# An attention kernel of two layers on one core: weights requested on another queue, fewer warm matmuls, new instruction orders

## The reference

```python
q = einsum('rc,bcn->brn', Wq, xf) + bq[None, :, None]     # 16 rows
k = einsum('rc,bcn->brn', Wk, xf) + bk[None, :, None]
v = einsum('oc,bcn->bon', Wv, xf) + bv[None, :, None]     # 128 rows
energy = einsum('bri,brj->bij', q, k)
attn = softmax(energy, axis=2)
out = einsum('bcj,bij->bci', v, attn)
x = gamma * out + x
```

## Time and profile before

| | |
|---|---|
| median of 3 runs | 193.89 us (193.38 to 194.21) |
| the profiled execution | 193.06 us |
| its span in the trace | 191.3 us |
| TensorE, ScalarE, GpSimd, VectorE busy | 94%, 81%, 82%, 76% of the span |
| DMA queue of SyncE | 9.31 MB, 16.7% of 16 engines' span |

### The profile page before, as it was taken

The page is one execution under the profiler, slowest core; times in us unless marked ns, Lnnn a source line. Parts: engine busy times, 40 slices in busy tenths (PEclk is TensorE's granted clock), DMA queues, the critical chain, the costliest instruction groups (busy, mean ns, idle before and its releaser), DMA issues.

```text
span 191.3 us, 3482 instructions
## 1 busy us (share of the span) xinstructions
PE 179.1 (94%) x1282; PEld 123.1 (64%) x1282; DVE 145.7 (76%) x137; ACT 155.5 (81%) x223; POOL 156.9 (82%) x120
## 2 busy tenths in 40 slices
PE   7889999799999989999998999999999999799993
PEld 2343445574798577877766786786668976565680
DVE  0258799868899898889878896798897867898241
ACT  2239969999999989999897998999998989348900
POOL 2267127989999999999999999999999976958760
PEclk9999999999999999999999999999999999999999
DMA  6920802200040040000400021003210101001111
GB/s 155 345 104 0 215 9 42 69 3 3 2 113 0 5 111 3 0 3 3 110 3 0 3 55 58 2 3 107 61 55 7 55 0 58 3 0 55 55 55 55
DMA packets 3890, 9.51 MB, mean 50 GB/s; under 512 B 548, under 2 KB 932, under 8 KB 3876
## 3 DMA queue, kind: packets, MB, share of 16 engines
q1 hardware_dynamic: 3876, 9.31, 16.7%
HBM read 2.89 MB, written 2.10 MB: 26 GB/s over the span
## 4 chain that ended last, share of the span: by engine, by line
PE 34%; POOL 31%; ACT 15%; issue 10%; DMA 4%; DVE 4%; SPq 1%; POOLq 0%; DVEq 0%; ACTq 0%
POOL attn_lo L364 14%; PE out_psum L720 10%; POOL attn_hi L359 9%; ACT ring L472 8%; PE out_psum L722 7%; ACT attn L484 4%; DMA qk_swapped<-qk 4%; PE ring L671 3%; PE ring L697 3%; PE out_psum L756 3%; PE ring L642 2%; DVE neg_max L563 2%; PE ring L624 2%; PE ring L657 2%; ACT attn_hi L490 2%
## 5 line engine op out<-in xcount | busy, mean ns | idle before, releaser
L364 POOL TENSOR_TENSOR attn_lo<-attn,attn_hi 128x1024 fp32r<-128x1024 f32 x37 | 90.4, 2455 | 1.8 <-ACT attn_hi L490 1.3
L563 DVE TENSOR_REDUCE neg_max<-ring 128x1 f32<-128x1024 f32 x64 | 75.6, 1219 | 15.7 <-PE ring L673 15.3
L472 ACT ACTIVATE ring<-ring,neg_max 128x1024 f32<-128x1024 f32 x64 | 69.6, 1087 | 9.9 <-DVE neg_max L563 9.3
L484 ACT ACTIVATE attn<-ring 128x1024 f32<-128x1024 f32 x64 | 63.3, 1024 | 9.8 <-DVE attn_lo L558 5.6
L359 POOL TENSOR_SCALAR attn_hi<-attn 128x1024 fp32r<-128x1024 f32 x35 | 39.2, 1134 | 5.5 <-ACT attn L484 5.4
L699 PE MATMUL ring<-qk_swapped,qk 64*128 64x512 f32 x64 | 29.0, 478 | 0.0
L697 PE MATMUL ring<-qk,qk_swapped 64*128 64x512 f32 x64 | 28.5, 468 | 0.3
L671 PE MATMUL ring<-qk_swapped,qk 64*128 64x512 f32 x56 | 25.1, 452 | 3.4 <-ACT attn L484 1.7
L673 PE MATMUL ring<-qk,qk_swapped 64*128 64x512 f32 x56 | 25.7, 461 | 0.0
L558 DVE TENSOR_TENSOR attn_lo<-attn,attn_hi 128x1024 fp32r<-128x1024 f32 x11 | 19.4, 1778 | 5.5 <-POOL attn_hi L359 4.7
L723 PE MATMUL out_psum<-attn_hi,v_hi 64*128 64x512 f32 x72 | 23.0, 399 | 0.0
(11 more groups left out here) (66 smaller groups left out, 358.1 us busy)
## 6 DMA issues: line engine op xcount, KB each, us to landing
qk_swapped<-qk SPq DMA_DIRECT2D x16, 256.0 KB, 3.7
out_dram<-x_all SPq DMA_DIRECT2D x8, 256.0 KB, 2.0
x_all<-x_in SPq DMA_DIRECT2D x3, 512.0 KB, 7.2
x_all<-x_in SPq DMA_DIRECT2D x2, 256.0 KB, 3.0
late<-late_in SPq DMA_DIRECT2D x1, 320.0 KB, 6.1
units<-units_in SPq DMA_DIRECT2D x1, 320.0 KB, 6.4
weights<-weights_in SPq DMA_DIRECT2D x1, 131.0 KB, 2.2
qk<-shift_rows SPq DMA_DIRECT2D x7, 8.0 KB
```

Of the source, the lines that this page charges most:

```text
L364: nc.gpsimd.tensor_tensor(attn_lo[:, k - 1], attn[:, k], attn_hi[:, k - 1].bitcast(fp32), ALU.subtract).then_inc(cut_made["lo", "gpsimd"], 1)
L472: nc.scalar.activation(e[:], e[:], ACT.Exp, bias=neg_max[s][:, i:i + 1], accum_out=row_sum[s][:, i:i + 1]).then_inc(sum_made, 1)
L484: nc.scalar.activation(attn[:, k], ring_tile("ET", s, k)[:].rearrange("p (a n) -> p a n", a=2), ACT.Exp).then_inc(attn_made, 1)
L563: nc.vector.tensor_reduce(neg_max[s][:, i:i + 1], ring_tile("E", s, i)[:], axis=AX.X, op=ALU.max, negate=True).then_inc(max_made, 1)
```

## The change

The request for the weights moves from SyncE's queue to ScalarE's, ahead of the loading of the activation table. `WARM_UP` goes from 10 to 5, and two of the eight `warm` words in the order have one pair in place of two. All five orders are new. The work is the same, but part of it changes engine:

| | GpSimd | ScalarE | VectorE |
|---|---|---|---|
| `hi` | 35 to 44 | 13 to 4 | |
| `lo` | 37 to 32 | | 11 to 16 |
| `v_hi` | 3 to 4 | 5 to 4 | |
| `v_lo` | 5 to 4 | | 3 to 4 |

In `POOL_ORDER`, the words from `parts.1.1` up to `parts.7.1` hold 28 `hi`, 29 `lo`, 3 `v_hi`, 4 `v_lo` before, and 33, 27, 2 and 3 after. In `DVE_ORDER`, those from `rows.1.1` to `rows.7.1` hold 5 `lo` and 2 `v_lo` before, 8 and 3 after. `PE_ORDER` has 7 E tiles between `shift.4.1` and `shift.5.1` before and 14 after, and behind `shift.7.1` 11 PH, 15 PV and 8 ET before, 9, 16 and 9 after.

```diff
-WARM_UP = 10
+WARM_UP = 5
...
 PE_ORDER = """
-raw.0.0.0 raw.0.1.1 E.0.6.2 QX.1.0.0 E.0.0.1 QK.1.0.0 E.0.7.2 warm.0.2 E.0.4.0 E.0.2.1 E.0.1.2 warm.0.2 E.0.3.0
-E.0.5.1 VX.0.0.2 warm.0.2 E.1.4.0 V.0.0.2 shift.0.0.1 warm.0.2 E.1.7.1 warm.0.2 QX.2.0.0 E.1.6.2 QK.2.0.0 warm.0.2
...
-shift.4.1.0 PH.3.3 E.5.2.0 PH.3.1 E.5.1.1 PV.3.3 PV.3.1 PV.3.2 QX.6.0.2 ET.4.3.0 QK.6.0.2 ET.4.2.1 PH.3.4 ET.3.7.0
-V.5.0.0 ET.4.0.1 PH.4.3 ET.4.6.2 PV.4.3 E.6.3.0 QX.7.0.1 shift.5.1.2 PV.4.0 ET.4.7.2 E.6.2.0 QK.7.0.1 PH.4.1 PH.4.2
...
-ET.6.7.1 ET.6.3.2 shift.7.1.0 PH.6.6 PH.6.4 PH.6.5 PH.6.3 PH.6.2 ET.7.3.0 ET.7.2.2 PV.6.2 PV.6.1 PV.6.3 PV.6.6
-PV.6.5 PV.6.4 ET.7.0.1 ET.7.1.0 ET.7.6.2 PV.6.7 PH.7.2 ET.7.5.1 ET.7.4.0 ET.7.7.2 PV.7.2 PH.7.3 PV.7.0 PH.7.1 PH.7.6
-PV.7.1 PV.7.3 PH.7.5 PH.7.4 PV.7.6 PV.7.5 PV.7.4 PV.7.7
+raw.0.0.0 raw.0.1.1 QX.1.0.2 E.0.2.0 QK.1.0.2 E.0.1.1 warm.0.2 E.0.6.2 E.0.7.0 E.0.0.1 warm.0.2 E.0.3.2 E.0.5.0
+E.0.4.1 warm.0.1 VX.0.0.2 E.1.4.0 V.0.0.2 shift.0.0.1 warm.0.2 E.1.5.1 warm.0.2 QX.2.0.0 E.1.0.2 QK.2.0.0 warm.0.1
...
+E.4.1.2 E.4.0.0 PV.2.5 PV.2.6 PV.2.4 PV.2.7 ET.3.0.1 ET.3.5.2 E.5.5.0 ET.3.4.1 PH.3.1 shift.4.1.2 PH.3.2 E.5.4.2
+ET.3.7.1 PV.3.2 PH.3.3 QX.6.0.0 E.5.6.1 ET.4.2.2 QK.6.0.0 PV.3.3 ET.4.1.2 PV.3.0 E.5.1.1 ET.4.3.2 PV.3.1 VX.4.0.0
+ET.4.0.2 V.4.0.0 ET.4.6.1 PH.3.6 E.5.2.2 PV.3.6 E.6.0.0 E.6.3.1 PV.3.7 E.6.1.2 PH.3.4 E.5.0.1 PH.3.5 E.5.7.0 PV.3.5
+PV.3.4 VX.5.0.2 ET.4.7.1 V.5.0.2 E.6.4.0 PH.4.3 E.5.3.1 PV.4.0 ET.4.5.2 E.6.7.0 PV.4.3 PH.4.1 E.6.2.2 PH.4.2 E.6.5.1
+PV.4.1 PV.4.2 QX.7.0.0 shift.5.1.2 QK.7.0.0 E.6.6.1 ET.4.4.2 PV.4.7 PH.4.6 ET.5.1.2 PV.4.6 ET.5.5.1 PH.4.4 ET.5.3.2
+ET.5.6.0 PH.4.5 ET.5.2.1 PV.4.4 shift.6.1.2 PV.4.5 ET.5.0.0 ET.5.4.2 ET.5.7.1 E.7.0.0 PV.5.0 ET.6.3.1 E.7.4.2 PH.5.1
...
+PV.5.4 E.7.2.0 E.7.1.1 PV.5.7 ET.6.6.2 PH.5.5 PV.5.6 PV.5.5 VX.7.0.0 ET.6.7.2 E.7.6.1 V.7.0.0 PH.6.6 PH.6.2 PH.6.4
+ET.6.5.2 shift.7.1.0 ET.6.1.1 PV.6.4 PV.6.7 PV.6.0 ET.7.5.0 ET.7.6.1 ET.7.4.2 PV.6.6 PH.6.5 PH.6.1 PV.6.5 ET.7.2.1
+ET.7.1.2 ET.7.7.0 PH.6.3 PV.6.1 PV.6.2 ET.7.0.2 ET.7.3.0 PV.6.3 PV.7.7 PH.7.6 PV.7.0 PH.7.3 PH.7.5 PH.7.4 PH.7.1
+PH.7.2 PV.7.1 PV.7.5 PV.7.3 PV.7.2 PV.7.4 PV.7.6
 """
 ACT_ORDER = """
-sum.0.6 evac.1.0 sum.0.0 sum.0.7 sum.0.4 sum.0.2 sum.0.1 sum.0.3 log.0.0 sum.0.5 sum.1.4 v_hi.0.0 log.0.1 sum.1.7
...
-sum.7.0 sum.7.4 sum.7.1 attn.5.4 sum.7.6 sum.7.3 attn.6.0 sum.7.2 attn.5.7 v_hi.6.0 attn.6.5 attn.6.2 sum.7.7
-attn.6.4 attn.6.1 attn.6.6 sum.7.5 log.7.1 hi.6.6 hi.6.4 attn.6.3 attn.6.7 attn.7.3 v_hi.7.0 attn.7.2 hi.7.2
-attn.7.0 attn.7.1 attn.7.6 attn.7.7 attn.7.5 attn.7.4 hi.7.5 hi.7.4
+evac.1.0 sum.0.2 sum.0.1 sum.0.6 sum.0.7 sum.0.0 sum.0.3 sum.0.5 log.0.0 sum.0.4 log.0.1 sum.1.4 sum.1.5 sum.1.0
+attn.0.1 attn.0.0 attn.0.3 attn.0.2 sum.1.3 attn.0.7 attn.0.4 sum.1.7 sum.1.1 sum.1.6 sum.1.2 sum.2.4 log.1.1
...
+v_hi.5.0 attn.4.4 sum.6.6 log.6.1 attn.5.1 attn.5.5 attn.5.3 attn.5.6 attn.5.2 attn.5.0 attn.5.7 attn.5.4 sum.7.0
+attn.6.3 sum.7.4 sum.7.5 sum.7.7 attn.6.2 sum.7.3 attn.6.0 v_hi.6.0 attn.6.4 sum.7.2 attn.6.6 sum.7.1 attn.6.7
+sum.7.6 log.7.1 attn.6.1 attn.6.5 attn.7.6 attn.7.4 attn.7.5 attn.7.1 attn.7.7 attn.7.0 attn.7.3 attn.7.2 hi.7.3
 DVE_ORDER = """
...
-max.6.6 finish.3.1 v32.5.0 max.6.3 rows.5.1 lo.4.2 max.6.2 mask.7.0 stack.7.0 finish.4.0 max.6.4 max.6.0 max.6.7
-max.6.5 max.6.1 finish.4.1 max.7.0 max.7.4 max.7.1 rows.6.1 max.7.6 max.7.3 finish.5.0 max.7.2 v32.6.0 lo.5.4
-max.7.7 v_lo.6.0 finish.5.1 max.7.5 v32.7.0 lo.6.5 rows.7.1 lo.6.6 lo.6.3 lo.6.4 finish.6.0 v_lo.7.0 lo.7.2
-finish.6.1 lo.7.6 lo.7.5 finish.7.0 finish.7.1
+max.0.2 max.0.1 max.0.6 max.0.7 max.0.0 max.0.3 max.0.5 max.0.4 max.1.4 rows.0.0 v32.0.0 max.1.5 max.1.0 mask.2.0
...
+v32.3.0 rows.3.1 max.4.5 max.4.6 max.4.2 lo.2.6 max.4.4 finish.2.0 mask.5.0 stack.5.0 max.4.7 max.4.1 max.4.0
+finish.2.1 max.5.5 rows.4.1 max.5.4 lo.3.6 max.5.6 mask.6.0 stack.6.0 max.5.1 finish.3.0 v32.4.0 max.5.2 max.6.3
+max.6.0 max.6.1 max.5.0 max.5.7 finish.3.1 max.6.4 v32.5.0 max.5.3 max.6.7 max.6.2 max.6.5 finish.4.0 rows.5.1
+max.6.6 mask.7.0 v_lo.5.0 stack.7.0 lo.4.4 lo.5.1 rows.6.1 finish.4.1 max.7.0 lo.5.3 max.7.4 max.7.5 max.7.7 lo.5.4
+finish.5.0 max.7.3 v32.6.0 max.7.2 max.7.1 v_lo.6.0 finish.5.1 max.7.6 v32.7.0 lo.6.6 rows.7.1 lo.6.2 lo.6.5
+v_lo.7.0 lo.6.1 finish.6.1 finish.6.0 lo.7.5 lo.7.1 lo.7.3 lo.7.4 finish.7.0 finish.7.1
 POOL_ORDER = """
-mask.1.0 stack.1.0 parts.0.0 parts.0.1 v_lo.0.0 hi.0.2 hi.0.3 hi.0.1 lo.0.2 lo.0.3 lo.0.1 parts.1.1 hi.0.6 lo.0.6
...
-hi.3.1 hi.3.2 lo.3.2 lo.3.3 parts.4.1 lo.3.1 hi.3.4 lo.3.4 lo.3.6 lo.3.5 hi.4.3 hi.4.2 v_lo.4.0 lo.4.3 hi.4.1
-parts.5.1 lo.4.1 v_hi.5.0 lo.4.6 lo.4.5 hi.5.1 hi.5.2 lo.4.4 hi.5.3 v_lo.5.0 lo.5.3 parts.6.1 lo.5.1 lo.5.2 hi.5.4
-hi.5.5 hi.5.6 lo.5.5 lo.5.6 hi.6.2 hi.6.1 hi.6.5 parts.7.1 lo.6.2 hi.6.3 lo.6.1 hi.7.3 lo.7.3 hi.7.1 lo.7.1 hi.7.6
-lo.7.4
+mask.1.0 stack.1.0 parts.0.0 parts.0.1 v_hi.0.0 v_lo.0.0 hi.0.1 hi.0.3 hi.0.2 lo.0.3 lo.0.2 hi.0.4 lo.0.4 parts.1.1
...
+hi.3.3 lo.3.2 hi.3.1 parts.4.1 hi.3.6 lo.3.3 lo.3.1 hi.3.5 hi.3.4 lo.3.4 hi.4.1 hi.4.2 lo.4.2 lo.3.5 v_lo.4.0 hi.4.6
+hi.4.3 lo.4.3 lo.4.1 lo.4.6 parts.5.1 hi.4.5 lo.4.5 hi.4.4 parts.6.1 hi.5.1 hi.5.3 hi.5.5 hi.5.2 hi.5.4 lo.5.2
+hi.5.6 lo.5.6 hi.6.3 lo.5.5 hi.6.2 hi.6.4 lo.6.3 hi.6.6 lo.6.4 parts.7.1 v_hi.7.0 hi.6.1 hi.6.5 hi.7.6 hi.7.5 lo.7.6
+hi.7.4 hi.7.2 hi.7.1 lo.7.2
 SP_ORDER = """
-swap.1.0 swap.0.0 place.0.0 swap.2.0 place.0.1 place.1.1 swap.3.0 place.2.1 swap.4.0 place.3.1 swap.5.0 place.4.1
...
+swap.0.0 swap.1.0 place.0.0 place.0.1 swap.2.0 place.1.1 swap.3.0 place.2.1 swap.4.0 place.3.1 swap.5.0 place.4.1
...
         @block.sync
         def _(sp):
-            sp.dma_start(weights[:], weights_in).then_inc(weights_loaded, 16)
             for h in range(2):
...
         @block.scalar
         def _(act):
+            act.dma_start(weights[:], weights_in).then_inc(weights_loaded, 16)
             act.preload_act_table_set("natural_log_exp_and_others")
```

52 lines of the change are left out of this document (21 added, 31 removed).

## The result

The changed kernel is slower: 196.05 us median (195.46 to 197.51), against 193.63 (192.99 to 194.21) for the kernel before in the same comparison, ratio 1.0143 [1.0111, 1.0176]. The prediction, 192.5 us and faster, had the wrong sign, and the time lies above its range. The profiled execution took 196.26 us, 3.2 more than the one before; its span is 194.2 us, 2.9 more than before.

A forecast was written before the change was run, and what follows sets the result against it. GpSimd's work was taken to set the middle, ScalarE close behind, and dependencies the head and tail. Head -0.7, middle from 119.0 to 120.7, tail -2.4 summed to -1.4, so 193.89 became 192.5 us; range 189.6 to 195.3.

The forecast's parts named there:

- end of `raw`: Head: with five pairs and the other queue, the first projection ends at 7.7 us, before 9.1; 1.4 us won.
- `raw` to first `hi`: Head: the new orders bring GpSimd's first `hi` to 28.1 us from 31.02, 2.9 us earlier in all.
- first `hi` to `parts.1.1`: GpSimd's four `hi`, three `lo`, 0.9 us of waiting and 1.0 for a collision put `parts.1.1` at 41.1 us.
- middle: From `parts.1.1` to `parts.7.1`: GpSimd's work +2.6 us, waits -0.9, so 120.7 us in place of 119.0.
- tail: From `parts.7.1` to TensorE's last matmul, 27.3 us before: 24.8 of work and 0.1 of gap, -2.4 us.
- the rate in the projection: Head: projection passes take 0.85 us from 3.7 until 4.8, then 0.43, and end at 7.7 us.
- the clock stays at 1.2 GHz through the projection: Rival, head: the rate does not rise at 4.8, passes end at 10.5, +2.8, 195.3 us; chance 0.06.
- My 3.7 for the arrival of half 0: Head: x's half 0, requested at 0.74 in place of 1.19, lands at 3.7 us, between 3.4 and 3.9.
- The bounds "0 and 0.45" for the queue: Head: of the 1.4 us won, the queue gives 0.2, at least 0 and at most 0.45.
- my units: Tail: TensorE's work behind `shift.7.1`, counted in matmuls of 0.23 us, is 23.1 us before and 23.3 after.
- VectorE's rival: Middle: VectorE's 11 two-input instructions wait for GpSimd's `lo`, the max behind them; over 4 us, 195.8 us; chance 0.13.
- the rival of bunched stages: Stages 5 and 6: 14 E tiles between two shifts give GpSimd 1.5 us of new waits; 193.9 us; chance 0.18.

The follow-up runs named there:

- e3: The kernel before with five warm pairs in place of ten: 193.28 us, ratio 0.9975.
- e2: The changed kernel with ten warm pairs in place of five, weights still on ScalarE's queue: 195.49 us, ratio 1.0104.
- e4: The kernel before with the weights requested on ScalarE's queue, ten pairs: 193.23 us, ratio 1.0005.
- e5: The changed kernel with eight warm pairs in place of five: 194.49 us, ratio 1.0063 to the kernel before.
- e1: The changed kernel with only its new orders: weights back on SyncE's queue, ten warm pairs: 195.63 us, ratio 1.0112 to the kernel before.
- e9: The kernel before with one word moved, `lo.3.6` from GpSimd to VectorE behind `max.5.1`: 195.60 us, ratio 1.0124.
- e7: e1 with three `hi` of stage 4 moved from GpSimd to ScalarE: 195.69 us, ratio 1.0126 to the kernel before.
- e8: e1 with `lo.4.4` and `lo.5.1` moved from VectorE back to GpSimd: 196.81 us, ratio 1.0182 to the kernel before.
- e11: e1 with `rows.6.1` one place earlier in VectorE's list, ahead of `lo.5.1`: 195.38 us, ratio 1.0103 to the kernel before.
- e12: e1 with a cut attention tile ahead of the native one in stage 0, `lo.0.3` ahead of `hi.0.2`: 195.84 us, ratio 1.0128 to the kernel before.
- e10: The kernel before with eight warm pairs and only the head of the new orders: 191.89 us, ratio 0.9926.

## Why the prediction was wrong

Its own intervals beside the measured ones (change against before, us of span):

| | predicted | measured | off |
|---|---|---|---|
| end of `raw` | -1.4 | +0.9 | 2.3 |
| `raw` to first `hi` | -1.5 | -1.2 | 0.3 |
| first `hi` to `parts.1.1` | +2.2 | +2.2 | 0 |
| middle | +1.7 | +1.6 | -0.1 |
| tail | -2.4 | -0.7 | 1.7 |
| sum | -1.4 | +2.9 | 4.3 |

**The step that failed most** is the rate in the projection: "From 3.7 to 4.8 passes go at 0.85 us (1.3 of them), the other 6.7 at 0.43: end at 7.7". The time of the rise, 4.8, was taken over from one execution in which TensorE ran without a break from 1.31 on. It is not a fixed time (4.3 to 6.6 in the twelve executions with eight or ten pairs). Behind five pairs and 0.82 us of nothing it came at 8.2, so that four to five of the eight passes went at 0.85. That is the rival "the clock stays at 1.2 GHz through the projection", which had 0.06: its mechanism is what happened, and its price (end at 10.5, +2.8) is near the 10.01. The gap was four times as long as the 0.2 that I gave it, because the weights landed after 3.7 us instead of 2.2 and became the last to arrive. My 3.7 for the arrival of half 0 came from an execution in which x was fast (2.7 us); in the four that request x at 0.74 it took 3.2 us or more, so that it was there at 3.9 at the earliest. The bounds "0 and 0.45" for the queue left out that the weights themselves come later: the projection could start at 4.45, against 4.21 in e3 with both on one queue. x alone varies by more than that, so a loss by the queue is not shown, and e2 and e4 show no gain. Eight pairs (e5) end this step at 8.34, and the time falls by 1.6 us: shown. Five pairs and the gap always went together, and no run parts them. The measured +0.9 is one execution against one, and before's own end of `raw` could have been 8.7 to 9.6.

**But the clock alone doesn't make the sign.** e5 is still at 1.0063, e1 at 1.0112: the orders themselves are slower. My terms without the first come to 0.0, e1's marks from the end of `raw` on to +1.8; nearly all of the difference is the tail's.

**Tail.** "I take 0.1 of gap: -2.4" was right about the gap and wrong about the size of the work. TensorE runs from the shift to the last matmul in 24.7 us without waiting, where my units gave 23.4 with the gap. The 76 product matmuls took 21.4 us in the chain, by my units 20.8; the nine `ET` and the switches to and from them make the rest. The same units had made before's work too small, so that "2.7 us were gaps" was about 1.3 in fact (its 23.1 scaled by 24.7/23.3 is 24.5, and 27.3 - 24.5 - 1.5 = 1.3), and before's timeline has one gap there, the 1.20 of the earlier trace rows: fewer gaps to win. Another 0.4 went between `parts.7.1` and the shift: VectorE's `lo` began at 163.29 and took 2.21 us, and the small subtraction at 164.37 took 1.19 for 0.20. I had counted such collisions in the middle and none here.

**Middle: the sum was right and its terms were not.** Predicted were +2.6 of work on GpSimd (own -2.1, collisions +4.7) and -0.9 of waits; measured are -0.4 and +2.0. With own work at -2.1, -0.4 leaves 1.7 for the collisions in place of 4.7: a new one can take the place of another, as in e9. (The bound "+3.8" should have been +3.9: 4 x 1.21 + 1.19 - 2.1.) VectorE's sixteen `lo` take 1.56 us in the mean where its eleven took 1.78, so they lost less time to GpSimd apiece, too. And where VectorE's instruction comes second, it waits as well. The waits are what I did not foresee. The sentence that failed is "So the middle is set by GpSimd's work", read from 96% busy. e7 takes 2.5 us off it (and puts 2.5 on ScalarE) for nothing, e9 takes 2.3 us off it and loses 2.4 (3.0 in its trace), and e8 adds 4.6 and loses 1.2. The busiest engine still waited, in turn for ScalarE's tiles, logs and `hi`, and more than two thirds of the changed kernel's waits for tiles in the middle stand in one place, behind `parts.6.1`.

**VectorE's rival** had the right mechanism, and e9 prices it: one two-input tile ahead of a `mask` was worth 2.4 us by its runs and 3.0 in its trace, far more than the 1.2 a piece I gave. At the two places that e8 and e11 tried in the new orders it is not what costs. So the rival is shown to exist, and not shown to be the cause of the 1.6.

**First `hi` to `parts.1.1`.** The sum of 13.0 was right by luck: 1.7 of waits stood for the 0.9, and no collision for the 1.0. That GpSimd alone sets it was wrong: ScalarE's log is 0.6 us ahead of `parts.1.1` in e1, and in e12 it is the log that is waited for.

**Right:** `raw` to first `hi` (20.4 predicted, 20.8 measured), and that the new head is a gain (e10 has 0.9 us of it with three moves). Right as well that nine `hi` less take 5 us off ScalarE in the middle (5.6). The Trainium skill (DMA: Bandwidth & Descriptors, "Issuing engines are not separate DMA queues") grants a second issuing engine no more than the issue time; e4 and e2 agree, with ratios that don't differ from those of the kernel before and of e1. The same skill (SBUF — State Buffer, "Who interferes with whom") has the two engines exclude each other and says that the order of issue decides who waits; I used the first half alone, and 2.80 us for VectorE's tile in e9 is the second.

**Open:** which words of the new orders make the middle 1.6 us longer. e7, e8, e11 and e12 each touch a visible wait, and none gives anything back. The stretch with 14 energy tiles between two shifts has TensorE at 34.78 of 35.22 us, and behind it the tiles of stage 5 come one behind the other and GpSimd waits 2.9 us for them. Both fit the rival of bunched stages ("1.5 us of new waits"), but no run spread the stages out.

## What to carry to other kernels

Let warm matmuls end when the data has landed, not before: the pairs cost nothing while TensorE waits, and behind five of them and a gap of 0.8 us the next eight passes took 1.9 us longer. Take a mark that moves between executions, like the rise of the clock, from several traces and not from one. When the lists of all engines are coupled in strict order, a busy share of 96% on one engine doesn't say that taking work off it helps: move one instruction first and look at what is queued behind it on the engine that gets it. And graft the part of a new order that is shown to win (here the head, 0.9 us, with eight pairs 191.89 us in all) instead of taking the whole.

## What the runs showed of the hardware

- The granted clock reads 1.00 from 4.0 to 8.4 us in the changed kernel, while passes start every 0.85 us up to 8.03, which is 1.2 GHz (0.43 is 2.4). The column does not show this state; the distance between weight loads does.
- Five pairs, then 0.58 or 0.82 us of idleness, then fp32 passes: the rise comes at about 9.2 (e3) or 8.2 (changed kernel). Eight or ten pairs with, by the rows, at most 0.12 us behind them: at 4.3 to 6.6 in twelve executions. Twelve runs of e3 spread over 4.5 us, 23 of before over 1.9.
- 131 KB of weights land 2.1 to 2.6 us after the request when they are asked for first on one queue (ten executions), 3.4 to 4.0 when x is asked for at the same moment on the other (four). The halves of x take 2.7 to 4.2 and 3.2 to 4.0.
- A VectorE `lo` that starts while GpSimd is in its own takes 2.80 us for 1.20 (e9); a GpSimd subtraction of 0.20 us that meets one of VectorE takes 1.19 (changed kernel, 164.37).
